# Reordering the weighting quarters and the second maximum in the first attention of a Perceiver block kernel (Trainium2, one core)

## The reference

```python
q = split_heads(layernorm(x) @ w_q.T + b_q)      # 16 heads of 16
k = split_heads(ctx @ w_k.T + b_k)               # ctx: 8 x 1024 x 256
v = split_heads(ctx @ w_v.T + b_v)
attn = softmax(q @ k.T / 4, axis=-1)
x = x + (attn @ v).reshape(B, 64, 256) @ w_o.T + b_o
```

## Time and profile before

| | us |
|---|---|
| median of 3 runs | 712.33 |
| lowest and highest run | 711.55, 713.86 |
| profiled execution, its own time | 712.5 |
| its span, first to last instruction | 710.7 |
| TensorE busy | 676.7 (95% of the span) |
| VectorE busy | 543.6 (76%) |
| GpSimd busy | 452.4 (64%) |
| ScalarE busy | 414.0 (58%) |

### The profile page before, as it was taken

The page is one execution under the profiler, slowest core; times in us unless marked ns, Lnnn a source line. Parts: engine busy times, 40 slices in busy tenths (PEclk is TensorE's granted clock), DMA queues, the critical chain, the costliest instruction groups (busy, mean ns, idle before and its releaser), DMA issues.

```text
span 710.7 us, 15537 instructions
## 1 busy us (share of the span) xinstructions
PE 676.7 (95%) x5712; PEld 554.0 (78%) x5712; DVE 543.6 (76%) x1212; ACT 414.0 (58%) x790; POOL 452.4 (64%) x487
## 2 busy tenths in 40 slices
PE   6899999999999988999999999998899899999998
PEld 3677778777777767999999999996457456666787
DVE  5887878787889776577777777754647999998676
ACT  3665656656665653566667667641336886665441
POOL 4848635546487644888998787736315699898130
PEclk9999999999999998999999999999999999999999
DMA  8301101011006565899999989975874610001000
GB/s 343 129 2 61 61 1 59 6 53 60 0 0 252 209 242 240 317 365 414 422 348 331 347 334 333 346 305 193 325 310 156 249 51 1 0 1 46 1 0 30
DMA packets 20365, 123.38 MB, mean 174 GB/s; under 512 B 2304, under 2 KB 6672, under 8 KB 13008
## 3 DMA queue, kind: packets, MB, share of 16 engines
q1 hardware_dynamic: 17376, 114.59, 42.0%
q0 software_dynamic: 2928, 8.00, 3.1%
HBM read 111.77 MB, written 10.81 MB: 172 GB/s over the span
## 4 chain that ended last, share of the span: by engine, by line
PE 81%; DVE 9%; ACT 5%; issue 3%; POOL 1%; DMA 1%; DVEq 0%; SPq 0%; ACTq 0%; PEldq 0%; POOLq 0%
PE banks L2279 70%; PE banks L2347 8%; DVE shown L2145 2%; PE banks L2911 2%; ACT probs L1155 1%; DVE negmax_raw L1674 1%; PE banks L2588 1%; ACT banks L1445 1%; DVE banks L2152 1%; DMA table<-in_table 1%; DVE xn L1566 1%; PE banks L2747 0%; ACT turned_back L1456 0%; POOL q_heads_hi L713 0%; POOL rstd L701 0%
## 5 line engine op out<-in xcount | busy, mean ns | idle before, releaser
L2279 PE MATMUL banks<-xT,raw 128*128 128x128 f32 x992 | 150.5, 275 | 0.6 <-DVE xT L1932 0.6
L2279 PEld LDWEIGHTS banks<-xT,raw 128*128 128x128 f32 x992 | 133.6, 191 | 3.1 <-issue 1.3
L971 POOL TENSOR_TENSOR w_lo<-raw,w_hi 128x1024 fp32r<-128x1024 f32 x52 | 122.8, 2389 | 0.9 <-ACT w_hi L1275 0.5
L1306 ACT ACTIVATE banks<-banks,later 128x128 f32<-128x128 f32 x208 | 70.5, 340 | 58.1 <-PE banks L2279 56.3
L1938 DVE CAST mid_hi<-banks 128x128 fp32r<-128x128 f32 x208 | 60.2, 289 | 36.5 <-ACT banks L1306 34.4
L1185 ACT ACTIVATE probsT<-banks 128x512 f32<-128x512 f32 x68 | 40.1, 598 | 74.8 <-PE banks L2347 74.5
L1055 POOL TENSOR_TENSOR inject<-BCbc,drive 128x1024 f32<-128x1024 f32 x31 | 72.8, 2362 | 11.3 <-DVE shown L2145 6.5
L1155 ACT ACTIVATE probs<-banks,negmax 128x1024 f32<-128x1024 f32 x64 | 71.2, 1113 | 11.7 <-DVE negmax L1676 9.9
L1674 DVE TENSOR_REDUCE negmax_raw<-banks 128x1 f32<-128x1024 f32 x64 | 77.5, 1211 | 0.4 <-PE banks L2279 0.3
L2279 PE MATMUL banks<-w_hi,mid_hi 128*128 128x256 f32 x208 | 75.5, 363 | 0.0
L2347 PE MATMUL banks<-table,probs 128*128 128x128 f32 x512 | 69.6, 279 | 0.4 <-DVE probsT L1647 0.4
(11 more groups left out here) (362 smaller groups left out, 1707.7 us busy)
## 6 DMA issues: line engine op xcount, KB each, us to landing
raw<-in_w SPq DMA_DIRECT2D x31, 2048.0 KB, 10.0
ctx_raw<-in_ctxT SPq DMA_DIRECT2D x8, 1024.0 KB, 4.7
ctxT<-in_ctxT SPq DMA_DIRECT2D x4, 2048.0 KB, 8.8
ctxN<-in_ctxN SPq DMA_DIRECT2D x4, 2048.0 KB, 13.9
x_slots<-zero SPq DMA_DIRECT2D x1, 3968.0 KB, 12.5
y_slots<-y_tile POOLq DMA_DIRECT2D x29, 128.0 KB, 7.0
wf<-in_w SPq DMA_DIRECT2D x9, 384.0 KB, 5.9
BCbc<-bc_rows SPq DMA_DIRECT2D x6, 512.0 KB, 6.9
```

Of the source, the lines that this page charges most:

```text
L971: nc.gpsimd.tensor_tensor(w2_lo[i % WB][:, cols], raw[i % WB][:, EW // 2:][:, cols], w2_hi[i % 2][:, cols].bitcast(F32), ALU.subtract).the ...
L1306: nc.scalar.activation(to, held, ACT.Gelu, bias=b1[:, bass.ds(at + u, 1)]).then_inc(gelu_done, 1)
L2279: return nc.tensor.matmul(o, lhsT, rhs, start=start, stop=stop)
```

## The change

On TensorE, in every duo of batches 0 to 6, both quarters now stand together behind the second turn, and the keys' projection is the last thing of the duo. The wait for the added tile moves with the quarters. On VectorE, in the same duos, the second maximum stands ahead of the values' addition. Nothing is added or taken away, and no order on ScalarE, GpSimd or SyncE is touched.

```diff
@@ VectorE, batch @@
                     elif later_one:
                         first_half(b - 1, 6)
+                    largest1(b, 2 * d + 1)
                     value_piece(value_at(b, d), par, d)
-                    largest1(b, 2 * d + 1)
@@ TensorE, batch @@
                     project_values(value_at(b, d), par, d)
-                    if d == DUOS - 1 and tile is not None:
-                        pe.wait_ge(tile_added, tile + 2)
-                    for which in quarters[2 * d]:
-                        weigh(*which)
                     if d:
                         turn(b, 2 * d - 1)
                     elif later_one:
                         turn(b - 1, 7)
+                    if d == DUOS - 1 and tile is not None:
+                        pe.wait_ge(tile_added, tile + 2)
+                    for which in quarters[2 * d] + quarters[2 * d + 1]:
+                        weigh(*which)
                     later_b, c, half = KEY_TURN[d]
                     project_keys(key_at(b, d), b + later_b, (par + later_b) % 2, c, half)
-                    for which in quarters[2 * d + 1]:
-                        weigh(*which)
```

## The result

The changed kernel took 718.96 us as a median of 5 runs (717.78 to 720.95), the kernel before 713.35 in the same comparison (711.55 to 716.26): ratio 1.0084, 95% interval 1.0063 to 1.0105, so 4.5 to 7.5 us slower. The forecast was 719.3, slower, with 0.89 for it. The profiled executions have spans of 717.2 and 710.7: 6.5 us apart.

A forecast was written before the change was run, and what follows sets the result against it. The prediction took TensorE to bound the attention before, and a chain through ScalarE and VectorE after. 4.5 + 1.9 + 1.1 - 0.5 = +7.0 on 712.5 gave 719.5, about 719.3 as a median; range on record 715.5 to 723.

The forecast's parts named there:

- The chain: Keys' end, ScalarE's high part, VectorE's low part, first maximum and first half, up to the second turn: 3.76 us after the scores.
- What follows the turn: TensorE from the second turn to the next scores: turn 1.00, quarters 0.44 + 0.57, keys 1.54, together 3.55 us.
- the stall: TensorE's wait at the second turn, ready at 3.28: 0.48 us in duos 0 and 2, 0.40 in duos 1 and 3.
- Batches 2 to 6: First attention, 20 duos: 10 at 7.31, 7 at 7.46, 3 at 8.1, 149.6 us against 145.1, so +4.5.
- Batch 1: Four duos, the first behind the S4 reciprocal at 8.46: together 30.7 us against 28.8, so +1.9.
- Batch 0: Three duos at +0.37 by the same chain or the values' one: +1.1 us, bounds 0 and 2.
- my own range: Forecast's own range, from batch 0, tail, and 0.05 either way in 23 duos: 716.3 to 722 us.
- The tail: Last batch: a normalisation of 2.07 us may shift against GpSimd's diagonals; -0.5 us taken, between nothing and -1.9.
- The swap: VectorE's second maximum ahead of the values' addition: addition done just before the keys need it, costs nothing, no cover.
- The drain: Changing TensorE's tiling mode drains it; four shape changes per duo instead of five, 0.11 us saved if TensorE is the bound.
- The first rival: In the first attention TensorE stays the bound and the change of shape is saved: 708 us, chance 7%.
- TensorE's busy time: Sign to look for: TensorE's busy time about the same, less 2 to 3 us.

The follow-up runs named there:

- experiment 3: Changed kernel with the first maximum of each duo taken over 512 of the 1024 keys; 708.79 us, 0.9951 to the kernel before.
- experiment 9: Changed kernel, VectorE's first half ahead of the first maximum, addition ahead of the second; ScalarE's order as in experiment 5; 711.39 us, 0.9990 to the kernel before.
- experiment 1: Changed kernel with VectorE in its old order (values' addition ahead of the second maximum), so TensorE's part alone; 718.16 us, 1.0079 to the kernel before.
- experiment 5: Changed kernel, quarters ahead of second turn; VectorE's old order; ScalarE's second exponential and keys' high part ahead of that turn's second half; 708.66 us, 0.9943 to before.
- experiment 2: Kernel before with only VectorE's second maximum moved ahead of the values' addition; 725.6 us, 1.0185 to the kernel before.
- experiment 4: Kernel before with the first maximum of each duo taken over 512 of the 1024 keys; 713.52 us, 1.0013 to the kernel before.
- experiment 6: As experiment 5 against the changed kernel, but without ScalarE's new order; 721.75 us, 1.0128 to the kernel before.
- experiment 7: Changed kernel with keys between the second turn and both quarters, and VectorE in its old order; 713.01 us, 1.0007 to the kernel before.
- experiment 8: Kernel before with the last batch's third-tile normalisation one instruction earlier on VectorE, ahead of a first half's copy; 711.68 us, 0.9990 to the kernel before.

## Why the prediction was right

*The chain.* It was 3.76 to the second turn in the forecast and is 3.74 in duo 0 of batch 2; its parts came out at 0.11 to the high part (0.12), 0.83 to the low part (0.84), 0.75 with the reciprocal, 1.32 and 0.84 from copy to turn. TensorE would have been ready at 3.27, by experiment 3 (3.28). What follows the turn took 3.59 and not 3.55. Over batches 2 to 6 duos 0 and 2 take 7.33 as a mean (7.31 forecast), the plain duos 1 and 3 7.48 (7.46), duo 3 with the projection 8.0 (8.1). Experiments 3 and 9 show that this is the cause: taking length out of the chain, by a shorter operation or by another order, takes the stall away with TensorE's stream unchanged.

*The sums.* Batches 2 to 6: 149.62, forecast 149.6. Batch 1: 30.69, forecast 30.7; its duo 0 behind the S4 reciprocal took 8.36 (8.46). Batch 0: +1.0 (+1.1), but this agreement is partly luck: I gave it to the chain or to the values' one, while the duos that carry it wait for the swapped addition (next but one paragraph). The lower end of my own range was added up wrongly: the three terms together give 715.6, not 716.3; nothing else hung on it.

*The tail* was the term that was mis-sized: -0.9 where I took -0.5 between 0 and -1.9. The 7.4 and the 0.9 make 6.5 up to the last scores (249.42 against 242.90). Behind them small differences cancel: the experts begin 6.9 later, and the spans are 6.5 apart again. The medians are 5.6 apart, within the interval.

*The swap.* That it costs nothing beside the new TensorE order was right for batches 2 to 6 (experiment 1, 0.01 us in 20 duos), and so was that it has no cover: alone it costs 1.85% against 0.84% for the whole change. It was wrong for batch 0, whose duos 0 to 2 have no quarters and so the same TensorE order in both kernels: there the swap costs 0.9 us in duos 1 to 3 (experiment 1). The costs of the two parts do not add, because the late addition is hidden by the waiting turn and the two quarters that the new order puts ahead of the keys.

*The drain.* The first rival rested on the rule that a change of the tiling mode drains TensorE (the Trainium skill, TensorEngine Tiling (Array Packing), Key Properties). The traces agree with it: with the chain out of the way duos 0 and 2 fall from 6.92 to 6.83 as a mean in experiment 3, and duo 0 to 6.81 or 6.82 in four of five batches of experiment 5, though duo 2 stays at 6.89 to 6.93 there. No run changes the number of shapes alone. The rival failed on the size: the 0.09 is less than a fifth of the 0.50 by which the stall lengthens the same duos.

*What was wrong.* I expected TensorE's busy time to fall by 2 to 3 us. In the window it is 144.76 against 144.39, and with the stall away 141.54 (experiment 3). At a stall the modelled end of the last matmul runs on into the idle time: the bracket says 0.33 where the starts say 0.47. So the saved switches don't show, and neither does about a third of the stall. Starts have to be compared with starts.

## What to carry to other kernels

An engine with a fifth of its time to spare can still set the pace: ask at which moment its work can begin, and which wait of the busy engine stands at the end of it. Before work is moved to the end of a period, add up what hangs on it (two engines' copies, whatever stands ahead in their queues, the next period's first buffer) against the distance to its consumer; here 3.76 against 3.28. If it doesn't fit, move the consumer back and not the producer forward: with the second turn behind the quarters, and the queue that feeds the next step reordered with it, keys last came out as a gain of 3.0 us in the window and not as a loss of 4.5. And ask the same where the period is shorter: in batch 0, without quarters, it was the harmless half of the change that cost.

## What the runs showed of the hardware

**A VectorE operation that waits out GpSimd's.** The normalisation of 128x256 takes either 0.40 to 0.41 us or about 2, depending on its start against GpSimd's 128x1024 product. It took 2.07 when it started 0.02 ahead (the same in experiments 2 and 4), 2.11 when it started 0.05 ahead (experiment 6), and 1.92 when it started 0.13 behind (experiment 7). It took 0.41 at 0.19 ahead (experiment 9) and at 0.28 ahead (experiment 5), and 0.40 or 0.41 from 0.53 ahead on. From experiment 7, VectorE and GpSimd:

```profile
227.57 1.92 DVE L1566 TENSOR_SCALAR xn<-X,moments,rstd 128x256 f32<-128x256 f32 x1
```

```profile
227.44 3.81 POOL L940 TENSOR_TENSOR tap_diag<-table,taps 128x1024 f32<-128x1024 f32 x2
```

In each slow case it ends 0.15 us behind the end of the first of the two products (half of the 3.81), so it waits for one product and not for both. By the Trainium skill (SBUF — State Buffer, two separate sides) whichever of the two starts first holds the shared ports. In experiment 7 that is GpSimd, and the trace agrees. In the other slow cases it would be VectorE by the starts that the profile shows, so at 0.02 to 0.05 us they don't tell who was first. That it is the ports, no run here shows by itself. A shift by some tenths of a microsecond in an unrelated stage changes the time by 0.9 us through such a pair.

**A half clock that sometimes reaches into a full stage.** Between the attention and the first experts, in the router and the sorting, the granted clock falls to half, 1.2 of 2.4 GHz. In the changed kernel TensorE ran 49 matmuls in the 6.8 us before the fall (262.4 to 269.2) and was busy for 6.07 of them; the attention has some 75 matmuls in as long a time. How long the clock stays down differs: 6.8 us (before, experiments 2 and 4), 10.2 (the changed kernel, experiments 1, 5, 7 and 8) or 13.6 (experiments 3, 6 and 9). The changed kernel, then experiment 6 (the fall alone, and the stage of the experts); the clock is the third number from the right:

```profile
269.20:279.50 10.30, 7.71 (x35) 7.39 (x36) 8.68 (x40) 5.44 (x10) 0.65 (x1) 0.50 0.98 420
```

```profile
271.10:284.70 13.60, 10.76 (x47) 10.08 (x47) 11.91 (x45) 5.76 (x11) 4.08 (x4) 0.50 0.82 343
280.49:495.81 215.32, 215.32 (x1777) 211.55 (x1778) 149.12 (x511) 131.29 (x302) 168.98 (x111) 0.99 0.88 336
```

In the changed kernel the clock is back at 279.5, before the experts begin at 280.46, and their stage takes 213.2 us. In experiment 6 it is back at 284.7, 4.2 us into the stage, which takes 215.3. Experiments 3 and 9 show the same (215.5 both), the other kernels 213.2 to 213.4. These 2.1 to 2.3 us lie behind the attention, and they explain most of why experiments 3 and 9 gained less in all than their windows say. With them experiment 6 is 6.8 + 2.1 = 8.9 slower by its span (719.6 against 710.7).

The length of the fall is not fixed by the kernel alone, as far as the mean granted clock of the timed executions tells, of which no trace is kept. Among those of the kernel before that were timed with the experiments the mean span is 710.3 at a mean clock of 0.992 or more and 712.1 below it; of the changed kernel 716.7 and 719.0; of experiment 9 708.3 and 711.4, six executions each. All executions of experiments 3 and 6 are below 0.992, and none of experiment 5. So a difference of 2 to 3 us between two medians can come from this alone; like with like, the changed kernel is 6.4 and 6.9 us slower. What decides how long the fall lasts was not tried.
